# A decoder block's values stage: the R tiles of a group set between the Y tiles of the second sequence

## What is computed

```
q = (x @ Wq + bq).reshape(Bx, Tx, N_Q, N_HEADS)      # 16 heads, width 128
k = (x @ Wk + bk).reshape(Bx, Tx, N_K, N_HEADS)
v = (x @ Wv + bv).reshape(Bx, Tx, N_V, N_HEADS)
q = transpose(q, (0, 3, 2, 1)); k = transpose(k, (0, 3, 1, 2)); v = transpose(v, (0, 3, 2, 1))
att = softmax(q @ k / sqrt(N_K), axis=-1)            # 128 x 128 a head: over channels
y = (att @ v) -> (Bx, -1, N_V * N_HEADS)
x = x + y @ Wo + bo
```

## Time and profile before

| what | value |
|---|---|
| median of 3 runs | 1157.07 us |
| profiled execution, its own time | 1157.29 us |
| its span in the trace | 1155.5 us |
| TensorE matmul busy | 1116.3 us (97%) |
| TensorE weight load busy | 938.2 us (81%) |
| VectorE busy | 749.4 us (65%) |
| ScalarE busy | 543.0 us (47%) |
| GpSimd busy | 468.6 us (41%) |
| granted TensorE clock | full in all 40 slices |

### The profile page before, as it was taken

How to read it: one execution, slowest core, us unless ns; L and a number is a source line. 1 busy time by engine, 2 the same in 40 slices (tenths; PEclk the granted TensorE clock), 3 DMA queues, 4 the chain that set the end, 5 groups by cost and what they waited for, 6 DMA issues and landing times.

```text
span 1155.5 us, 15845 instructions
## 1 busy us (share of the span) xinstructions
PE 1116.3 (97%) x5816; PEld 938.2 (81%) x5816; DVE 749.4 (65%) x1376; ACT 543.0 (47%) x1129; POOL 468.6 (41%) x412
## 2 busy tenths in 40 slices
PE   4999999999999999999999999999999999999998
PEld 4888888878888878888888878778787878787886
DVE  6555547787757678765425344689867876887532
ACT  2455673324142366577415223177627762775130
POOL 1222326441332275664344030066517751775131
PEclk9999999999999999999999999999999999999999
DMA  7456544534334633312631022361024111410000
GB/s 237 134 183 182 172 167 150 170 122 168 124 123 129 192 91 127 93 37 90 236 109 40 34 98 52 140 189 47 2 81 129 47 47 46 120 46 1 38 1 36
DMA packets 54375, 122.19 MB, mean 106 GB/s; under 512 B 10025, under 2 KB 10025, under 8 KB 52250
## 3 DMA queue, kind: packets, MB, share of 16 engines
q1 hardware_dynamic: 54298, 121.18, 32.2%
HBM read 103.32 MB, written 17.84 MB: 105 GB/s over the span
## 4 chain that ended last, share of the span: by engine, by line
PE 84%; DVE 8%; ACT 4%; issue 3%; POOL 1%; DMA 0%; POOLq 0%; DVEq 0%; SPq 0%
PE bank L158 18%; PE bank L159 18%; PE bank L160 18%; PE bank L565 6%; PE bank L566 6%; PE bank L525 4%; PE bank L580 4%; PE bank L581 4%; PE bank L547 2%; PE bank L548 2%; PE bank L535 2%; PE bank L536 2%; POOL wal L1979 1%; DVE x1d L733 1%; DVE xmx L749 1%
## 5 line engine op out<-in xcount | busy, mean ns | idle before, releaser
L565 PE MATMUL bank<-x3h,w 128*128 128x512 f32 (+2 forms) x364 | 142.8, 395 | 1.5 <-DVE x3l L836 1.3
L566 PE MATMUL bank<-x3l,w 128*128 128x512 f32 (+2 forms) x364 | 139.8, 386 | 0.0
L1407 ACT ACTIVATE yh<-bank 128x512 fp32r<-128x512 f32 x64 | 38.1, 599 | 211.7 <-PE bank L160 211.7
L1979 POOL TENSOR_TENSOR wal<-raw_a,wah 128x512 fp32r<-128x512 f32 x44 | 60.6, 1405 | 116.8 <-ACT wah L1429 116.7
L158 PE MATMUL bank<-wah,gh 128*128 128x512 f32 x256 | 104.0, 406 | 2.8 <-POOL wal L1979 1.3
L917 POOL TENSOR_SCALAR pe_x<-pe_x,xri,gam 128x512 f32<-128x512 f32 x96 | 75.0, 782 | 72.2 <-DVE xri L753 69.4
L1984 POOL TENSOR_TENSOR wbl<-raw_b,wbh 128x512 fp32r<-128x512 f32 x64 | 88.1, 1401 | 36.0 <-ACT wbh L1449 35.7
L158 PE MATMUL bank<-yh,rh 128*128 128x512 f32 x256 | 100.2, 392 | 2.5 <-DVE xacc L1839 2.5
L1675 DVE TENSOR_TENSOR yl<-bank,yh 128x512 fp32r<-128x512 f32 x64 | 44.0, 691 | 88.1 <-ACT yh L1407 88.1
L158 PE MATMUL bank<-wah,ph 128*128 128x512 f32 x256 | 100.4, 392 | 0.3 <-POOL wal L1979 0.3
L159 PE MATMUL bank<-wal,gh 128*128 128x512 f32 x256 | 100.2, 391 | 0.0
(11 more groups left out here) (172 smaller groups left out, 3023.2 us busy)
## 6 DMA issues: line engine op xcount, KB each, us to landing
raw_a<-in_wk SPq DMA_DIRECT2D x8, 1024.0 KB, 5.5
raw_b<-in_wq SPq DMA_DIRECT2D x8, 1024.0 KB, 5.2
raw_a<-in_wo SPq DMA_DIRECT2D x8, 1024.0 KB, 5.1
raw_b<-in_wvt SPq DMA_DIRECT2D x8, 1024.0 KB, 4.9
ternary_scratch<-wraw SPq DMA_DIRECT2D x24, 341.2 KB, 3.0
x1d<-x_scratch SPq DMA_DIRECT2D x48, 128.0 KB, 3.0
kd<-in_ctx SPq DMA_DIRECT2D x48, 128.0 KB, 3.0
w<-ternary_scratch SPq DMA_DIRECT2D x2, 2730.0 KB, 10.8
```

The costliest lines, as they stand in the source:

```text
L565: pe.matmul(u_bank[w][0:m, cols], lhs, x3h[:, c, cols], start=c == 0, stop=False)
L566: mm = pe.matmul(u_bank[w][0:m, cols], lhs, x3l[:, c, cols], start=False, stop=c == CK - 1)
L1979: pool.tensor_tensor(wal[:, c, :], raw_a[:, c, :], wah[:, c, :].bitcast(F32), ALU.subtract).then_inc(s["wal_pool"], 1)
```

## The change

Between the four Y tiles of sequence 1 stand now R tiles 0, 1, 2, then 3, 4, 5, then 6, 7, and none behind the last. The same order is written for the banks, for TensorE, ScalarE and VectorE. What stood behind the eight R tiles moves too: `dve_weight_means` to behind the first three R tiles, `dve_bias_v` and `act_matrix` to behind the last two. `dve_between` stays behind each Y tile of sequence 1, but the R tiles that follow this Y tile now come ahead of it. `act_rows` of the next pass (group 3 of pass 0) now comes ahead of all R tiles.

```diff
+R_AFTER = (0, 1, 2), (3, 4, 5), (6, 7), ()
@@ attention_tiles
             for c in range(CK):
-                for hp in range(2):
-                    yield "R", p, j, c, hp
-            for c in range(CK):
                 yield "Y", p, j, 1, c
+                for r in R_AFTER[c]:
+                    yield "R", p, j, r // 2, r % 2
@@ pe_y
                 pe_y_tile(pe, p, j, i, c, range(TJ))
+                if i:
+                    for r in R_AFTER[c]:
+                        pe_r(pe, p, j, r)
@@ pe_r: one tile a call; its two waits only where r == 0
-        def pe_r(pe, p, j):
-            pe.wait_ge(s["ptl"], GROUPS * p + j + 1)
-            pe.wait_ge(s["wbl"], CK * load(p, GROUPS + j + 1))
+        def pe_r(pe, p, j, r):
+            if r == 0:
+                pe.wait_ge(s["ptl"], GROUPS * p + j + 1)
+                pe.wait_ge(s["wbl"], CK * load(p, GROUPS + j + 1))
@@ act_values
-                for c in range(CK):
-                    for hp in range(2):
-                        act_high(act, rh[:, c, hp, :], A["R", p, j, c, hp])
                 if last and further:
                     act_rows(act, p + 1, 0)
-                if not last:
-                    act_matrix(act, p, j + 1)
                 for c in range(CK):
                     act_high(act, yh[:, 1, c, :], A["Y", p, j, 1, c])
+                    for r in R_AFTER[c]:
+                        act_high(act, rh[:, r // 2, r % 2, :], A["R", p, j, r // 2, r % 2])
+                    if c == 2 and not last:
+                        act_matrix(act, p, j + 1)
@@ dve_values
                 for c in range(CK):
-                    for hp in range(2):
-                        dve_low(dve, rl[:, c, hp, :], rh[:, c, hp, :], A["R", p, j, c, hp])
-                if p == 0 and j == 0:
-                    dve_weight_means(dve, link)
-                if not last:
-                    dve_bias_v(dve, p, j + 1)
-                for c in range(CK):
                     dve_low(dve, yl[:, 1, c, :], yh[:, 1, c, :], A["Y", p, j, 1, c])
+                    for r in R_AFTER[c]:
+                        dve_low(dve, rl[:, r // 2, r % 2, :], rh[:, r // 2, r % 2, :], A["R", p, j, r // 2, r % 2])
+                    if p == 0 and j == 0 and c == 0:
+                        dve_weight_means(dve, link)
+                    if c == 2 and not last:
+                        dve_bias_v(dve, p, j + 1)
                     dve_between(dve, link, p, j, c)
```

More of the change, by code:

```diff
@@ L1337, in pe_y_early @@
                     pe_ret(pe, early, 0, last, 1)
-        def pe_r(pe, p, j):
-            pe.wait_ge(s["ptl"], GROUPS * p + j + 1)
-            pe.wait_ge(s["wbl"], CK * load(p, GROUPS + j + 1))
-            for c in range(CK):
-                for hp in range(2):
[L1344 to L1351, removed]
+        def pe_r(pe, p, j, r):
+            if r == 0:
+                pe.wait_ge(s["ptl"], GROUPS * p + j + 1)
+                pe.wait_ge(s["wbl"], CK * load(p, GROUPS + j + 1))
+            c, hp = divmod(r, 2)
+            u = A["R", p, j, c, hp]
+            pe_bank(pe, u)
+            for h in range(2):
+                col = slice(256 * h, 256 * (h + 1))
+                head, rows_ = 2 * hp + h, slice(c * P, (c + 1) * P)
+                mm = three_passes(pe, a_bank(u)[:, col], wbh[:, head, rows_], wbl[:, head, rows_],
+                                  pth[:, hp, col], ptl[:, hp, col], True, True)
+            mm.then_inc(s["a_ready"], 1)
         def pe_out(pe, p, j, i, a):
@@ L1374, in pe_values @@
                     pe_t(pe, p, GROUPS - 1)
-                pe_r(pe, p, j)
                 pe_y(pe, p, j, 1)
@@ L1877, in dve_values @@
                 for c in range(CK):
-                    for hp in range(2):
-                        dve_low(dve, rl[:, c, hp, :], rh[:, c, hp, :], A["R", p, j, c, hp])
-                if p == 0 and j == 0:
-                    dve_weight_means(dve, link)
-                if not last:
-                    dve_bias_v(dve, p, j + 1)
-                for c in range(CK):
-                    dve_low(dve, yl[:, 1, c, :], yh[:, 1, c, :], A["Y", p, j, 1, c])
+                    dve_low(dve, yl[:, 1, c, :], yh[:, 1, c, :], A["Y", p, j, 1, c])
+                    for r in R_AFTER[c]:
[4 more added lines that the diff above has]
+                        dve_bias_v(dve, p, j + 1)
                     dve_between(dve, link, p, j, c)
```

## The result

| | before | after |
|---|---|---|
| median of 4 runs | 1157.13 us (1156.56 to 1157.32) | 1163.8 us (1163.38 to 1164.15) |
| profiled execution | 1157.29 us, span 1155.5 | 1163.67 us, span 1161.9 |
| TensorE matmul busy | 1116.3 us | 1119.0 us |
| VectorE busy | 749.4 us | 756.2 us |

The change makes the kernel 6.7 us slower, ratio 1.0058 (1.0041 to 1.0076). I had predicted 1160.0 and a range up to 1162.3: the direction was right, the size was not.

What follows compares the result with a forecast made beforehand. The prediction took TensorE's matmuls plus its stops to bound the kernel. Its terms, 2.5 + 0.4 + 0.6 - 0.6 + 0.1 + 0 = +3.0 us on the median of 1157.07, gave 1160.0 us, range 1157.8 to 1162.3.

Steps and rivals of the forecast that it cites:

- The Newton steps in group 2 of pass 1: Last four still start within GpSimd's first split operation and end with the fourth; +0.1 us, between -1.1 and +1.3.
- part 1: Group 0 of pass 0, means and first ternary step: VectorE waits for GpSimd's reduction, TensorE stops at Y tile 2; +2.5 us.
- the race in group 1 of pass 0: VectorE's wlow against GpSimd's split, held back by the matrix: if won, additions come earlier; -0.6 us, between -1.1 and 0.
- Part 2: Changes of tile kind, both passes: each added switch back from 256 to 512 columns costs 0.02 to 0.03 us; +0.4 us.
- Part 3: Values stages, three places: VectorE work now falls beside GpSimd's matrix subtraction and may wait; +0.6, -0.6 and +0.1 us.
- Group 2 of pass 0: Ternary step beside GpSimd's matrix subtraction delays wraw and perhaps the second output addition; +0.6 us, between 0 and 1.6.
- the long wait: VectorE beside the matrix subtraction waits for all that operation has left, about 2.2 us, against 0.92 at least.
- Part 4: The rest, including ScalarE's work, the stop on e_x and later x1d loads: 0 us, at most 0.5 for the loads.
- GpSimd's long operation holds VectorE: Rival, group 2 of both passes: VectorE waits out GpSimd's operation; 5.8 us at most, 4.5 middle, 1161.6 us; chance 0.2.
- the second place: Newton steps in group 2 of pass 1, said to be quantised by GpSimd's split and hardly move; +0.1 us.
- Slower: Whole kernel: the measured time lies above the line at 1159.4 us; chance 0.66.
- The late loads: Rival, stage after pass 1: x1d lands at 729 or later, stopping TensorE 1 to 3 us; 1162 us; chance 0.03.

Runs made afterwards that it cites:

- Experiment 1: Changed kernel with the means and first ternary step of group 0 of pass 0 moved from behind R tile 2 to behind R tile 5: 1160.51 us, ratio 1.0028.
- experiment 4: Kernel before with one more Newton-like multiplication behind the last four steps of group 2 of pass 1: 1160.0 us, ratio 1.0025.
- 6: Changed kernel with R tiles spread in pass 1 only, pass 0 with eight in a row: 1160.5 us, ratio 1.0023.
- 7: Changed kernel with all eight R tiles in a row again, dv and the matrix copy left behind Y tile 2: 1161.0 us, ratio 1.0035.
- experiment 8: Kernel before with two more statistics instructions behind the last Newton steps of group 2 of pass 1: 1160.58 us, ratio 1.003.
- experiment 2: Changed kernel with four Newton steps of group 2 of pass 1 moved from behind R tile 7 to behind R tile 5: 1159.12 us, ratio 1.0018.
- 5: Changed kernel with R tiles spread in pass 0 only, pass 1 in the order of before: 1161.3 us, ratio 1.0034.
- experiment 9: Kernel before with VectorE's side work behind the last Y tile of sequence 1 put ahead of that tile's subtraction: 1154.74 us, ratio 0.9972.
- 10: Changed kernel, means/ternary step and four Newton steps behind R tile 5, side work ahead of the last Y tile's subtraction: 1156.11 us, ratio 0.9985.

## Why the prediction was right or wrong

Four steps of the sum failed. The Newton steps in group 2 of pass 1 had +0.1 and cost +1.25; the delay that part 1 leaves in VectorE's queue had no term and cost +1.05; the race in group 1 of pass 0 had -0.6 and gave nothing (+0.05); the clock had no term and cost 1.6 us in the profiled execution.

**Part 1 was right** in mechanism and size: 2.6 measured for 2.5, VectorE idle 2.63 us for about 2.3, the means at 177.08 for 177.33. Experiment 1 shows that this term hangs on the place of the means alone. What was missing is what comes behind. I ended the term with the stop and took VectorE's delay as used up there. But the delay stayed in VectorE's queue, and the ternary steps behind it met GpSimd's additions (1.75 and 1.69 us for 0.65) and then the matrix (2.67 us). That cost +1.05 us, for which the sum had no term.

**Part 2 was right.** A Y tile behind R tiles takes 2.748 us from start to start and another 2.72, so 0.03 a switch and 0.4 in all.

**Part 3 failed**, in two of its three places. *Group 2 of pass 1*, +0.1, because the last four would start 0.8 us later but still within the first split operation, was the term that was most wrong. I had written down both ends of the bound, and the far one, +1.3 for one missed split operation, is what happened (+1.25; experiment 4 gives +1.22 for one step). The error was in counting: with the third step held to the end of the matrix and the split following at once, the fourth step can only run behind the first split operation, and the last four then begin in the second. My 0.8 us left the fourth step out. *Group 1 of pass 0*: the race was lost, not won, 0 instead of -0.6. The matrix began at 236.85 and lasted 2.40 us, and the split followed it at once, 1.42 us behind the first output matmul (239.19 against 237.77), before 1.39. It was held back by 0.03 us, not by the 0.1 or more that I had, and `wlow` came 0.09 us behind it. My own two numbers, 4.2 and 4.3, already had `wlow` last, and I priced the term as half won all the same:

```profile
239.19 6.21 POOL L1982 TENSOR_TENSOR wal<-raw_a,wah 128x512 fp32r<-128x512 f32 x4
```

```profile
239.28 1.68 DVE L1933 TENSOR_SCALAR wlow<-wraw,wthr 105x832 f32<-105x832 f32 x1
```

*Group 2 of pass 0* was right: 0.33 for 0.6, by the path that I had worked out for the long wait. `wraw` took 3.11 us instead of 1.08, and the second addition ended 11.1 us behind E where I had 11.5. I had let this case go up to 1.6, though, and the 0.6 was a middle between both waits: that it came near is in part luck.

```profile
287.28 0.65 DVE L1933 TENSOR_SCALAR wlow<-wraw,wthr 105x832 f32<-105x832 f32 x1
287.96 3.11 DVE L1935 SCALAR_TENSOR_TENSOR wraw<-wraw,wthr,wlow 105x832 f32<-105x832 f32 x1
```

GpSimd's matrix stands at 287.59 with 2.59 us. By the Trainium skill ("SBUF — State Buffer", section "SBUF: two separate sides") the loser blocks for the whole instruction; the traces agree, now also for the operation of 2.4 us (2.34 and 2.27 us waited for Newton steps of 0.16).

**Part 4 was right**: `x1d` came late, at 733.88 with a DMA wait of 1.88 us, the addition behind it at 734.34, and TensorE shows no stop there (the first 60 matmuls of that block take 13.607 us, 13.605 before). The stop on `e_x` stayed at 1.1.

**The clock had no term at all.** The rows of before showed full clock in all 40 slices with a stop of 1.7 us, and I took the price of a stop to be its length. With one of 2.9 the profiled execution also paid 1.6 us at half clock. Between the spans the miss is 6.4 - 3.0 = 3.4 us: 1.6 for the clock, 1.15 for the missed split operation, 1.05 for the tail of part 1, 0.65 for the race and 0.1 in part 1, less 0.3 in group 2 of pass 0 and 0.8 outside the values stages' blocks.

**The rivals.** The one whose mechanism came nearest is "GpSimd's long operation holds VectorE" (1161.6), for which I had 0.2. Even at its full 5.8 us, 1162.9, it stays below the 1163.8 measured. Its argument against itself, that the second place hardly moves, was the same miscount. My own sum with the missed operation (1.15), the tail (1.05) and the race lost (0.65) would have been 1162.9, still above the range. The clock's 1.6 leads beyond the 1163.8 measured, and the 0.3 and 0.8 above bring it back. Slower was the outcome to which I gave the most (0.66), and it came. The late loads (1162) are nearer in number only, and no stop of theirs is there. The range was too narrow upwards: it stopped at 1162.3, inside the case of the long waits, and had nothing for the clock.

**What stays open** is what decides in a single execution whether the clock falls behind such a stop. In the profiles it fell behind a stop of about 3 us in the kernel after and in experiments 1, 6, 7 and 8 in group 2 of pass 1, and behind the `yl` stop in 2 and 5; it did not in experiment 4 with 2.91 shown, nor behind the `yl` stop of 2.33 in the kernel after; the one in experiment 2 was only 1.85. In experiments 2, 4, 5, 9 and 10 it fell in a later stage too, behind two short stops in a row (1.1 and 0.5 to 0.9 us shown), which the kernel before also has, in its profile without a fall. Among the 27 runs of before in the first set, 11 have a mean clock a little below 1.0, and these are the slower ones (1157.7 to 1159.0). Where in those executions it fell is not recorded; the later stages are one such place. So the length of a single stop alone doesn't decide, and I can't give the chance of a fall for a length of stop.

## What to carry to other kernels

Work that is moved to another place is priced by what it stands beside there, on the other engine too: here the largest costs came from a subtraction on GpSimd and steps of VectorE that were both off the critical path and had been apart. Where small steps each wait for one operation of another engine, count them one by one against its operations, and where the count could be one more, take the full price. Put side work ahead of the operation that has slack, not behind it, and before the other engine starts: four lines did that here and won 3.0 us, where the spread order with the same repair and two more won 1.6. And when a stop of TensorE gets near 3 us, add a further 1.6 us with a chance, for the clock.

## What the runs showed of the hardware

- A VectorE step of 128x4 (0.16 us) behind GpSimd's 128x1024 subtraction (2.39 us) takes 2.34 us, behind one of 128x512 (5.04 / 4 = 1.26 us) 1.22 us: what it waits for sets its time, not its own size. `bn_stats`, with one operand, took 0.71 us a piece beside GpSimd's split (experiment 8), against 0.69 elsewhere, so it hardly waits.
- One stop of TensorE of some 3 us, amid matmuls back to back, was followed by 3.4 us at 1.2 GHz, in which a matmul of 512 columns costs 0.43 us instead of 0.227; with a fall it costs 1.6 us more than its length. The same stop in experiment 4 was not, and in experiment 9 the half clock came behind stops of 1.15 and 0.47 us.
- In the stop itself the granted clock is full (681.00 to 684.20), and the half clock is shown only when TensorE is busy again. One has to look behind a stop to find its second half.
